# Causal attention masked while turned weights are copied, with the whole program's order laid out from new costs

## The reference

```python
dot = jnp.einsum('bhid,bhjd->bhij', q, k)
scores = dot * dot / (q_norm_sq + k_norm_sq.transpose(0, 1, 3, 2) - 2.0 * dot + EPSILON)
mask = jnp.triu(jnp.ones((Lq, Lq)), k=1) * -1000000000.0
attn = jax.nn.softmax(scores + mask[None, None, :, :], axis=-1)
out = jnp.einsum('bhij,bhjd->bhid', attn, v).transpose(0, 2, 1, 3).reshape(Bq, Lq, E)
return out @ w_out + b_out
```

## Time and profile before

| | us |
|---|---|
| median of 3 runs | 5082.77 (5076.04 to 5086.52) |
| time of the profiled execution | 5068.32 |
| its span, first to last instruction | 5066.3 |
| PE busy | 4401.1 (87%) |
| DVE busy | 3392.7 (67%) |
| ACT busy | 2583.0 (51%) |
| POOL busy | 2323.3 (46%) |

### The profile page before, as it was taken

The page is one execution under the profiler, slowest core; times in us unless marked ns, Lnnn a source line. Parts: engine busy times, 40 slices in busy tenths (PEclk is TensorE's granted clock), DMA queues, the critical chain, the costliest instruction groups (busy, mean ns, idle before and its releaser), DMA issues.

```text
span 5066.3 us, 65767 instructions
## 1 busy us (share of the span) xinstructions
PE 4401.1 (87%) x23008; PEld 2677.9 (53%) x23008; DVE 3392.7 (67%) x7648; ACT 2583.0 (51%) x5513; POOL 2323.3 (46%) x2203
## 2 busy tenths in 40 slices
PE   7888888999999999987787777777799999999997
PEld 3444445555555555554554454444555555555564
DVE  4454466666666666647889988999766666656553
ACT  4344344444444444427887777777444444444442
POOL 1111145455454454534555555565545444455441
PEclk9999999999999999997777777887899999999998
DMA  2000000000001000000000000100000000000000
GB/s 65 9 5 5 9 22 11 3 3 5 20 3 31 7 9 11 16 16 17 20 20 17 16 22 18 32 11 15 29 3 3 5 20 9 25 15 17 11 15 21
DMA packets 61208, 77.56 MB, mean 15 GB/s; under 512 B 13896, under 2 KB 45264, under 8 KB 60880
## 3 DMA queue, kind: packets, MB, share of 16 engines
q1 hardware_dynamic: 60880, 73.36, 5.0%
HBM read 35.61 MB, written 12.58 MB: 10 GB/s over the span
## 4 chain that ended last, share of the span: by engine, by line
PE 61%; DVE 21%; issue 7%; ACT 6%; POOL 4%; DMA 1%; SPq 1%; DVEq 0%; POOLq 0%; ACTq 0%
PE wide L725 44%; PE o_ps L725 8%; PE turn_ps L728 5%; PE wide L728 3%; DVE prob L1262 3%; DVE x L1256 2%; DVE pt L1299 2%; DVE prob L1273 2%; DVE hid L1256 1%; DVE x L1143 1%; DMA shifted<-resid 1%; DVE st L1280 1%; ACT pt L1106 1%; POOL rn L1443 1%; DVE w_up L1239 1%
## 5 line engine op out<-in xcount | busy, mean ns | idle before, releaser
L1477 POOL TENSOR_SCALAR prob<-prob,st 128x256 f32<-128x256 f32 (+1 forms) x1024 | 524.8, 533 | 976.9 <-DVE st L1286 976.6
L725 PE MATMUL wide<-x,w_up 128*128 128x512 f32 (+5 forms) x2560 | 943.5, 593 | 21.6 <-DVE k_t L1203 11.4
L725 PE MATMUL wide<-w_in,x_t 128*128 128x512 f32 (+1 forms) x1792 | 828.9, 607 | 6.5 <-DVE w_up L1246 3.1
L725 PE MATMUL o_ps<-pt,v 128*64 128x256 f32 (+2 forms) x5632 | 619.7, 369 | 118.6 <-DVE pt L1299 77.0
L1106 ACT ACTIVATE pt<-turn_ps 128x512 f32<-128x512 f32 x384 | 229.2, 597 | 854.1 <-PE turn_ps L728 854.1
L725 PEld LDWEIGHTS o_ps<-pt,v 128*64 128x64 f32 (+1 forms) x5632 | 394.6, 140 | 380.1 <-issue 191.2
L1075 ACT ACTIVATE prob<-prob,st 128x256 f32<-128x256 f32 (+1 forms) x1024 | 479.0, 472 | 194.7 <-DVE st L1273 194.5
L728 PE MATMUL turn_ps<-ident,prob 128*128 128x128 f32 x2816 | 465.3, 285 | 125.6 <-ACT pt L1106 121.9
L725 PEld LDWEIGHTS wide<-x,w_up 128*128 128x128 f32 (+2 forms) x2560 | 365.1, 200 | 375.5 <-issue 354.4
L728 PEld LDWEIGHTS turn_ps<-ident,prob 128*128 128x128 f32 x2816 | 315.1, 142 | 420.1 <-issue 238.0
L725 PEld LDWEIGHTS wide<-w_in,x_t 128*128 128x128 f32 x1792 | 339.9, 200 | 370.4 <-issue 363.8
(11 more groups left out here) (132 smaller groups left out, 7823.2 us busy)
## 6 DMA issues: line engine op xcount, KB each, us to landing
kept<-resid SPq DMA_DIRECT2D x16, 512.0 KB, 2.6
x<-kept SPq DMA_DIRECT2D x16, 512.0 KB, 3.3
w_up<-hid SPq DMA_DIRECT2D x64, 128.0 KB, 2.2
x<-hid SPq DMA_DIRECT2D x64, 128.0 KB, 2.3
shifted<-resid SPq DMA_DIRECT2D x32, 224.0 KB
w_in<-in_f_wqkv SPq DMA_DIRECT2D x4, 1536.0 KB, 6.4
w_up<-in_f_w SPq DMA_DIRECT2D x4, 1364.0 KB, 6.3
resid<-in_x SPq DMA_DIRECT2D x8, 512.0 KB, 8.1
```

Of the source, the lines that this page charges most:

```text
L725: return eng.matmul(out, lhsT, rhs, start=start, stop=stop, skip_group_check=True)
L1477: last = eng.tensor_scalar(pr[:, local_span(t)], pr[:, local_span(t)], sm[:, 8 + t:9 + t], 1.0, ALU.mult, ALU.mult)
```

## The change

Three things are done.

1. In stage b the part `mask` is gone. The turned weights have keys on the partitions and queries on the columns, so the same triangle, turned (`causal_keep`), is applied by `pt_b` on DVE as it copies from PSUM: a product instead of a copy. The turns now wait for `exp`.
2. For that, all blocks on the diagonal must be in DVE's bank. `B_TURNS` lists for each kind of step the blocks (head, key block) of the first and the second bank, and `turned_to` tells `mix` where a block went. ACT's bank has 2, 4 and 4 blocks, DVE's 4, 2 and 4; the first `B_OWN` = 4, 2, 2 of these are masked, and a third kind of step needs a second DVE instruction, a plain copy.
3. The costs in `cost()` are replaced for nearly all parts of all stages, so `ordered()` lays out all queues and PSUM places anew.

```diff
+B_TURNS = [([(0, 0), (1, 0)], [(0, 1), (0, 2), (1, 1), (1, 2)]),
+           ([(0, 0), (0, 1), (1, 0), (1, 1)], [(0, 2), (1, 2)]),
+           ([(0, 0), (0, 1), (1, 0), (1, 1)], [(0, 3), (1, 3), (0, 2), (1, 2)])]
+B_OWN = [4, 2, 2]
+def turned_to(i, k, block):
+    for half in range(2):
+        if (k, block) in B_TURNS[i % 3][half]:
+            return 512 * half + P * B_TURNS[i % 3][half].index((k, block))
...
-B_COST = {"bclip": (0.15, 0.27), "bnum": (0.1, 0.22), "bguess": (0.2, 0.47), "bclose": (0.2, 0.6), "bmul": (0.8, 0.6),
-          "exp": (0.85, 0.21), "turn_a": (0.03, 0.175), "turn_b": (0.03, 0.175), "pt_a": (0.06, 0.12),
-          "pt_b": (0.12, 0.135), "mix": (0.05, 0.34), "mask": (0.95, 0.0)}
+B_COST = {"bclip": (0.3, 0.27), "bnum": (0.1, 0.23), "bguess": (0.2, 0.48), "bclose": (0.2, 0.58), "bmul": (0.8, 0.78),
+          "exp": (0.85, 0.24), "mix": (0.05, 0.33)}
...
-        return 2.8 if i % 2 else 0.0
+        return {"score": {"a": 1.92, "f": 1.72}, "mix": {"a": 2.4, "f": 1.68}}[kind][st] if i % 2 else 0.0
+    if kind in ("turn_a", "turn_b", "pt_a", "pt_b") and st == "b":
+        n = len(B_TURNS[i % 3][kind[-1] == "b"])
+        return {"turn": 0.03 + 0.17 * n, "pt_a": 0.1 + 0.12 * n, "pt_b": (0.26 if i % 3 == 2 else 0.13) + 0.135 * n}[
+            "turn" if kind[0] == "t" else kind]
...
-        "low": {"a": 1.3, "f": 2.2}, "exp": {"a": 1.6, "f": 2.9}, "inv": {"a": 0.9, "f": 0.15}, "wt": {"a": 1.2, "f": 2.2},
-        "turn_a": {"a": 0.6, "f": 0.6}, "turn_b": {"a": 0.6, "f": 0.45}, "pt_a": {"a": 0.65, "f": 0.65},
-        "pt_b": {"a": 0.65, "f": 0.6}}
+        "low": {"a": 1.22, "f": 1.87}, "exp": {"a": 1.78, "f": 2.65}, "inv": {"a": 0.68, "f": 0.17},
+        "wt": {"a": 0.98, "f": 2.08}, "turn_a": {"a": 0.62, "f": 0.5}, "turn_b": {"a": 0.62, "f": 0.42},
+        "pt_a": {"a": 0.6, "f": 0.6}, "pt_b": {"a": 0.69, "f": 0.55}}
...
-    flat = {"xt": 1.2, "qk": 3.6, "vv": 3.6, "spread": 1.2, "aq": 3.6, "lat": 1.8, "ak": 1.8, "av": 1.8, "bqkv": 3.7,
-            "bk": 0.8, "bq": 0.8, "proj": 1.9, "xt2": 1.2, "up_g": 3.6, "up_h": 3.6, "down": 2.8,
...
-            "gelu": 5.6, "bn_h": 2.4, "nrm_h": 1.3, "cos": 1.4, "ss": 1.5, "join": 2.7, "k_c": 0.65, "ak_c": 1.25,
...
-            "bn_f": 1.0, "bn_f2": 1.8, "nrm_f": 1.9, "xt2_c": 1.4, "gate": 1.5, "hid": 1.6, "res2": 1.3,
+    flat = {"xt": 0.95, "qk": 3.7, "vv": 3.7, "spread": 0.93, "aq": 3.7, "lat": 1.85, "ak": 1.9, "av": 1.9, "bqkv": 3.7,
+            "bk": 0.65, "bq": 0.65, "proj": 1.72, "xt2": 1.06, "up_g": 3.55, "up_h": 3.55, "down": 2.6, "sel": 0.65,
...
+            "gelu": 5.6, "bn_h": 2.3, "nrm_h": 1.5, "cos": 2.08, "ss": 1.62, "join": 2.63, "k_c": 0.68, "ak_c": 1.23,
...
+            "bn_f": 1.11, "bn_f2": 1.79, "nrm_f": 2.9, "xt2_c": 1.6, "gate": 1.49, "hid": 1.49, "res2": 1.23,
...
-            put("mask", k, at + 1 / steps, final("exp", k))
             for side in "ab":
-                put("turn_" + side, k, at + 2 / steps, final("mask", k))
+                put("turn_" + side, k, at + 2 / steps, final("exp", k))
...
-                    pe.wait_ge(S["mask"], nth("mask", u, i))
-                    at, to = (0, 0) if kind == "turn_a" else (b_width(i), 512)
-                    for kb in range(b_width(i) // P):
-                        last = tr(ps[:, to + kb * P:to + (kb + 1) * P],
-                                  prob[SLOTS[u, i]["prob"]][:, at + kb * P:at + (kb + 1) * P])
+                    pe.wait_ge(S["exp"], nth("exp", u, i))
+                    for k, block in B_TURNS[i % 3][kind == "turn_b"]:
+                        to, at = turned_to(i, k, block), k * b_width(i) + block * P
+                        last = tr(ps[:, to:to + P], prob[SLOTS[u, i]["prob"]][:, at:at + P])
...
-                    w = {"f": 384, "a": 512, "b": b_width(i)}[stage_of(u)]
-                    ps = wide[PLACE["turn_b", u, i]][:, 512:1024] if stage_of(u) == "b" else turn_ps
-                    eng.tensor_copy(pt[:, 512:512 + w], ps[:, 0:w]).then_inc(S["pt_b"], 1)
+                    if stage_of(u) == "b":
+                        ps, met, n = wide[PLACE["turn_b", u, i]], P * B_OWN[i % 3], P * len(B_TURNS[i % 3][1])
+                        last = eng.tensor_tensor(blocks(pt[:, 512:512 + met]), blocks(ps[:, 512:512 + met]),
+                                                 causal_keep[:, :].unsqueeze(1).to_broadcast([P, met // P, P]), ALU.mult)
+                        if n > met:
+                            last = eng.tensor_copy(pt[:, 512 + met:512 + n], ps[:, 512 + met:512 + n])
+                        last.then_inc(S["pt_b"], 1)
+                    else:
+                        w = {"f": 384, "a": 512}[stage_of(u)]
+                        eng.tensor_copy(pt[:, 512:512 + w], turn_ps[:, 0:w]).then_inc(S["pt_b"], 1)
...
-                elif kind == "mask":
...
-                    eng.tensor_tensor(at, at, ones, ALU.mult).then_inc(S["mask"], 1)
```

More of the change, by code:

```diff
@@ L90 @@
         "DVE": "bn_h nrm_h cos ss join k_c ak_c row bss bclip bmul low inv pt_b out_b res bn_f bn_f2 nrm_f xt2_c gate hid res2",
-        "POOL": "rstd_h sin rn brow bias_b bclose mask wt rstd_f bias back rot pad_out pad_down pad_v",
+        "POOL": "rstd_h sin rn brow bias_b bclose wt rstd_f bias back rot pad_out pad_down pad_v",
         "SP": "load_in load_out load_rot load_up kept moved back_in store dup_a dup_b"}.items():
@@ L109, in cost @@
     if kind in ("bden", "bdot"):
-        return 0.05 + 0.38 * b_width(i) / P if kind == "bdot" else 0.0
+        return 0.05 + 0.34 * b_width(i) / P if kind == "bdot" else 0.0
     by_stage = {
-        "low": {"a": 1.3, "f": 2.2}, "exp": {"a": 1.6, "f": 2.9}, "inv": {"a": 0.9, "f": 0.15}, "wt": {"a": 1.2, "f": 2.2},
-        "turn_a": {"a": 0.6, "f": 0.6}, "turn_b": {"a": 0.6, "f": 0.45}, "pt_a": {"a": 0.65, "f": 0.65},
-        "pt_b": {"a": 0.65, "f": 0.6}}
[3 rows of a table added]
     if kind in by_stage:
         return by_stage[kind][st]
-    flat = {"xt": 1.2, "qk": 3.6, "vv": 3.6, "spread": 1.2, "aq": 3.6, "lat": 1.8, "ak": 1.8, "av": 1.8, "bqkv": 3.7,
-            "bk": 0.8, "bq": 0.8, "proj": 1.9, "xt2": 1.2, "up_g": 3.6, "up_h": 3.6, "down": 2.8,
-            "xt_c": 1.3, "raw": 2.2, "v_c": 1.1, "q_c": 0.7, "aq_c": 1.1, "lat_c": 0.6, "av_c": 1.1, "bsq": 1.3,
-            "bk_c": 0.65, "bq_c": 0.65, "out": 0.7, "olog": 1.4, "sel": 0.6, "out_b": 2.1,
-            "gelu": 5.6, "bn_h": 2.4, "nrm_h": 1.3, "cos": 1.4, "ss": 1.5, "join": 2.7, "k_c": 0.65, "ak_c": 1.25,
-            "row": 1.1, "bss": 0.9, "res": 1.3,
-            "bn_f": 1.0, "bn_f2": 1.8, "nrm_f": 1.9, "xt2_c": 1.4, "gate": 1.5, "hid": 1.6, "res2": 1.3,
-            "rstd_h": 1.2, "sin": 3.4, "rn": 3.4, "brow": 3.0, "bias_b": 2.5,
-            "rstd_f": 1.2, "bias": 2.5, "back": 2.5, "rot": 4.0, "pad_out": 1.0, "pad_down": 0.3, "pad_v": 4.0}
+    flat = {"xt": 0.95, "qk": 3.7, "vv": 3.7, "spread": 0.93, "aq": 3.7, "lat": 1.85, "ak": 1.9, "av": 1.9, "bqkv": 3.7,
+            "bk": 0.65, "bq": 0.65, "proj": 1.72, "xt2": 1.06, "up_g": 3.55, "up_h": 3.55, "down": 2.6, "sel": 0.65,
+            "xt_c": 1.2, "raw": 2.04, "v_c": 1.03, "q_c": 0.6, "aq_c": 1.03, "lat_c": 0.6, "av_c": 1.03, "bsq": 0.93,
+            "bk_c": 0.57, "bq_c": 0.57, "out": 0.6, "olog": 1.2, "out_b": 2.4,
+            "gelu": 5.6, "bn_h": 2.3, "nrm_h": 1.5, "cos": 2.08, "ss": 1.62, "join": 2.63, "k_c": 0.68, "ak_c": 1.23,
+            "row": 0.95, "bss": 0.8, "res": 1.23,
+            "bn_f": 1.11, "bn_f2": 1.79, "nrm_f": 2.9, "xt2_c": 1.6, "gate": 1.49, "hid": 1.49, "res2": 1.23,
+            "rstd_h": 1.02, "sin": 3.14, "rn": 3.05, "brow": 1.8, "bias_b": 2.4,
+            "rstd_f": 1.01, "bias": 2.38, "back": 2.5, "rot": 4.0, "pad_out": 1.0, "pad_down": 0.3, "pad_v": 4.0}
     return flat.get(kind, 0.2)
@@ L487 @@
         "aq aq_c lat lat_c ak ak_c av av_c bqkv row bsq bv bss brow bk bk_c bq bq_c bias_b "
-        "score bden bdot low inv exp wt wt_b bclip bnum bln bguess bclose binv bmul turn_a turn_b mask neg pt_a pt_b mix sel out olog oexp osum out_b "
+        "score bden bdot low inv exp wt wt_b bclip bnum bln bguess bclose binv bmul turn_a turn_b neg pt_a pt_b mix sel out olog oexp osum out_b "
         "proj res moved bn_f bn_f2 var_f rstd_f nrm_f bias xt2 xt2_c up_g gate gelu up_h hid down res2 back_in back store "
@@ L516, in build @@
         causal_floor = sb("causal_floor", P)
-        causal_ones = sb("causal_ones", P)
+        causal_keep = sb("causal_keep", P)
         sum_rows = sb("sum_rows", P)
@@ L1652, in constants @@
         "local_mask": np.concatenate([previous, own], axis=1),
-        "causal_floor": np.where(j > i, DEN_MAX, DEN_MIN), "causal_ones": np.where(j > i, 0.0, 1.0),
+        "causal_floor": np.where(j > i, DEN_MAX, DEN_MIN), "causal_keep": np.where(i > j, 0.0, 1.0),
         "sum_rows": np.where(i == j - j % BROW + BHD, 1.0, 0.0),
```

6 lines of the change are left out of this document (3 added, 3 removed).

## The result

The changed kernel takes 4961.67 us (4 runs, 4955.91 to 4968.62) where the kernel before took 5079.41 us beside it. The ratio is 0.9772, with a 95% interval of 0.9754 to 0.979. That is 118 us, where 119 were forecast. The profiled execution has a span of 4953.9 us. That the sum came so close is partly luck: terms that were too small and a term that did not come cancelled, as far as the experiments can separate them.

What follows compares the result with a forecast made beforehand. DVE was taken to bound the causal stage and PE the others. Terms -77 (blocking) + 9 (copies) - 16 (bclose idle) - 7 (idle share) - 28 (order) = -119 us, from 5083 to 4964 us; overall range 4880 to 5050.

Steps and rivals of the forecast that it cites:

- Where it would happen and what bounds it: DVE bounds the causal stage, busy 1155.23 of 1280 us (90%); PE bounds the feed-forward stages and leads the first.
- -77 us for the mask's blocking: Causal stage: 35% of 221 us by which POOL blocks DVE's two-input products goes with the mask; bounds 0 and 221.
- Rival (b): Causal stage: blocking moves, DVE's products meet bclose as often as both before; the 77 us fall away, 5041; chance 0.12.
- +9 us for the copies: Causal stage: masked copies and dealt blocks cost DVE 141 ns more a round over 64 rounds; bounds 0 and +20.
- -16 and -7 us for waits: Causal stage: 16 of DVE's 24.0 us idle for bclose, and 7 us idle share of the shortened stage, are saved.
- -28 us for the order: New planner costs close PE's gaps: 20 us over 32 feed-forward units, 8 us in the first stage.

Runs made afterwards that it cites:

- Run 9: The kernel before in its own order, with POOL's mask product replaced by three fills reading no SBUF: 5000.25 us against 5072.84, ratio 0.9848.
- Run 8: The changed kernel with plain copies in place of the masked ones, same blocks and order: 4959.83 us.
- run 1: The changed kernel's code with the old planner costs, so masked copies and dealt blocks only: 4975.51 us, ratio 0.9795.
- run 2: The kernel before with the new planner costs and nothing else, mask still on POOL: 5073.75 us against 5077.9, ratio 0.9993.
- run 3: The changed kernel with one extra SBUF-reading POOL product behind each closing product in the causal stage: 5010.94 us.
- run 4: The changed kernel with two or three extra POOL fills, reading nothing, behind each closing product in the causal stage: 4975.3 us.
- run 6: The changed kernel with POOL's closing product also waiting for DVE's products of the step before, in planner and program: 4965.96 us, ratio 0.9773.
- run 7: The changed kernel with the planner's old per-block price for DVE's products, 0.6 instead of 0.78: 4970.36 us.
- run 10: The changed kernel in its own order with POOL's closing product replaced by fills of nearly the same length: 4867.47 us, ratio 0.9594.
- run 11: The changed kernel with closing product tied behind DVE's products of the step before in the planner's list only, no wait in the program: 5006.55 us.
- Run 5: The changed kernel with both copies of turned weights in the feed-forward stages cut to their first 128 columns: 4928.54 us.
- run 12: The changed kernel without the inverse's correction (closing product and DVE's L1272 product left out), lower planner price for bmul: 4827.09 us, ratio 0.9519.

## Why the prediction was right, step by step

**Where it would happen and what bounds it: right.** The causal stage gave all of it. DVE's busy time per unit fell from 144.6 to 128.7 us, its idle time stayed (15.3 and 16.7).

**-77 us for the mask's blocking: the mechanism right, the time about right, the size of the blocking too small.** Run 9 measured 73 us, with nothing else changed. But the products lost 123 us of blocking in that run, not 77: the mask's own share went (about 80 us by its overlap with long products in the trace before), and they also met the closing product less often. DVE gave part of it back as idle time, 15.3 to 20.2 us a unit. So 77 and 73 agree because two things that I did not foresee offset each other. Rival (b), that blocking moves over to the closing product, had the wrong sign.

**+9 us for the copies: the busy time came as worked out** (123 for 113.5 us). Run 8 leaves nothing to see for the mask itself.

**-16 and -7 us for waits: wrong in the place, too small in the sum.** DVE's wait for the closing product did not fall by 16 us, it rose from 24.0 to 46.5, and the idle time that I let shrink with the stage rose from 15.3 to 16.7 us a unit. Still the shorter chain was worth something. The edit alone gave 102 us where my terms without the order make 91. Taking run 9's 73 and the copies' +9 from it leaves 38 us for the shorter chain and the freed queue of POOL, where I had 23. This is a difference between two runs with two orders, so an estimate. The trace shows where it lies: with the mask's blocking gone and its chain kept (run 9) DVE idles 20.2 us a unit, with the chain shortened (run 1) 15.0. Its copies wait less for the transposes; these are the waits of run 9 in 2300:3510 and of run 1 in 2300:3480:

```profile
DVE pt L1299 <- PE wide L728: 41.5, 44, 2.1
...
DVE pt L1312 <- PE wide L742: 18.0, 23, 1.5
```

**-28 us for the order: the step that failed.** I booked 20 us in the feed-forward stages and 8 in the first. The feed-forward pace is 92.1 to 92.3 us in runs 1 to 4, 6 to 8, 10 and 11 as in both kernels (91.8 in run 9, in the old order), and the first stage did not move. PE's idle time did not shrink, it grew. It is 64 us in 1000:2000 of the changed kernel, where the kernel before had 53, and the three waits below make nearly all of it; the wait for ACT's copy, which I thought other work could cover, had been 22.9 us there:

```profile
PE turn_ps L745 <- ACT pt L1122: 31.0, 22, 2.1
PE wide L742 <- ACT sq L1018: 19.7, 11, 1.8
PE wide L742 <- DVE hid L1394: 12.9, 11, 1.2
```

PE's busy time for the same 408 matrix instructions of a unit fell as its gaps grew, from 87.3 us busy and 4.9 idle to 86.3 and 5.8. The granted clock of that stretch accounts for the busy part: 0.99 in the three runs with the old costs (the kernel before, runs 1 and 9), 1.00 in all others, and 87.3 x 0.99 = 86.4. So the new order even gave PE 1 us a unit back, some 30 us over 32 units, and the pace did not follow. A busy share of 95% did not mean that less busy time shortens the unit; PE's gaps grew by as much, and no run shows why. That the new costs sum to the measured 87 us was true and worth nothing. What the new order gave was 14 us, between run 1 and the changed kernel, whose ranges just touch; in their traces the causal stage is 15 us shorter. On the old code the same costs gave nothing (run 2), so this is no fixed worth of the costs. The 15 us by which the chain was under-priced and the 14 by which the order was over-priced cancel in the sum: that part of 118 against 119 is luck. One figure of the working is off as well: 10.2 us a round in the new plan less the 9.2 left after the removal (10.4 - 1.2) is 1.0, not 1.2, and in the changed kernel the products take 8.4. No term rests on it.

**Left open.** Why two different orders give one feed-forward pace to 0.2 us, and why the granted clock there is 0.99 with one and 1.00 with the other. Run 5 shows that copies of half the duration recover some 0.7 us a unit, so most of PE's 5 to 6% of gaps is not set by them. No run separated the rest. The first stage of runs 3 and 4, 11 to 12 us later, is not explained either; runs 5 and 10, which left that stage alone too, are 5 to 6 us later there. How much of run 10's gain is the shorter fills was not separated.

## What to carry to other kernels

Price an instruction on POOL by whom it blocks as well as by who waits for it: here nobody waited much for the mask (PE, 34.9 us in the largest group) and it cost 73 us in run 9. Compare the mean of DVE's two-input products with their minimum; if they differ, find the POOL instructions that run beside the long ones, and move the work into an instruction that reads PSUM anyway. An explicit wait that keeps the two apart removes the blocking and can give it all back as idle time, and better costs in a list scheduler gave nothing by themselves here (run 2). A busy share near 95% does not show that less busy time would shorten a unit: PE's fell by 1 us of 87 in the feed-forward stages and the pace stayed.

## What the runs showed of the hardware

A fill on POOL does not block DVE's products, a product of the same length does: 187 us of fills lengthened them by 6 us, 171 us of products by 68. A product of a PSUM and an SBUF operand started inside a product of POOL and kept its 0.41 us. PE's granted clock in the causal stage, a mean over the window, was 0.78 before, 0.81 after the change and 0.88 in run 12, with PE's busy share at 75, 79 and 83%. In the feed-forward stretch it was 0.99 with the old costs and 1.00 with the new. I had left the clock out of the sum, and no run separated what it was worth in the causal stage.
